# Adding the last routed batch into the output by accumulating transfers, unit by unit, instead of gathering it at the end

## What is computed

```python
x = x + 0.5 * _L1_ffn_ref(_layernorm(x, axis=-1), gate_w, w1, w2, w3)   # the last block, then return x

# _L1_ffn_ref: 8 experts, the 2 best of each token, at most 320 tokens of a batch for each expert
dispatch = einsum('bsm,bsec->ebcm', hidden_states, dispatch_mask)
h1 = einsum('ebcm,emh->ebch', dispatch, w1)
h3 = einsum('ebcm,emh->ebch', dispatch, w3)
expert_out = einsum('ebch,ehm->ebcm', silu(h1) * h3, w2)
final = einsum('ebcm,bsec->bsm', expert_out, combine_mask)
```

## Time and profile before

| | |
|---|---|
| median of 3 runs | 875.42 us (875.26 to 875.46) |
| the profiled execution's own time | 876.98 us |
| its span, first to last instruction | 875.2 us |
| PE busy in the span | 740.4 us (85%) |
| DVE, ACT, POOL busy | 503.7, 551.9, 322.5 us |
| mean granted clock of TensorE | 0.948 |

### The profile page before, as it was taken

How to read it: one execution, slowest core, us unless ns; L and a number is a source line. 1 busy time by engine, 2 the same in 40 slices (tenths; PEclk the granted TensorE clock), 3 DMA queues, 4 the chain that set the end, 5 groups by cost and what they waited for, 6 DMA issues and landing times.

```text
span 875.2 us, 13632 instructions
## 1 busy us (share of the span) xinstructions
PE 740.4 (85%) x4304; PEld 393.6 (45%) x4304; DVE 503.7 (58%) x1483; ACT 551.9 (63%) x960; POOL 322.5 (37%) x352
## 2 busy tenths in 40 slices
PE   5799999989999879858889797998988958789981
PEld 1432222212232225535555464775766845456650
DVE  6876532115655748622657299786897957223341
ACT  5368987989989866422466776867867515234440
POOL 3090003301001424263123475664763831634343
PEclk9899999999999999988999998998999969889996
DMA  4057651621881211111210200000000011111313
GB/s 127 1 194 177 146 118 46 224 67 49 293 171 53 85 42 39 36 45 36 71 35 18 68 1 1 1 1 1 1 1 1 31 47 30 56 38 51 91 44 92
DMA packets 63372, 57.55 MB, mean 66 GB/s; under 512 B 8260, under 2 KB 51385, under 8 KB 63040
## 3 DMA queue, kind: packets, MB, share of 16 engines
q1 hardware_dynamic: 57888, 47.84, 19.7%
q0 software_dynamic: 5120, 8.68, 3.0%
q10 hardware_dynamic: 288, 0.10, 0.0%
HBM read 28.64 MB, written 29.05 MB: 66 GB/s over the span
## 4 chain that ended last, share of the span: by engine, by line
PE 29%; DVE 11%; issue 8%; POOL 6%; ACT 4%; DMA 2%; another core or an unknown queue 2%; SPq 0%; POOLq 0%; DVEq 0%; ACTq 0%
PE ps_main L1628 11%; PE ps_main L1658 7%; PE ps_side L1946 3%; DVE mb_act L1982 2%; PE ps_main L2014 1%; POOL moe_slots L1555 1%; PE ps_main L1589 1%; PE ps_main L1624 1%; DVE moe_hid L1653 1%; POOL mb_z L2158 1%; DMA moe_back<-moe_rows 1%; POOL mb_y_in L2156 1%; PE ps_main L1699 1%; POOL mb_h_dec L2100 1%
## 5 line engine op out<-in xcount | busy, mean ns | idle before, releaser
L685 ACT ACTIVATE attn_p<-attn_ps 128x1024 f32<-128x1024 f32 x256 | 240.6, 1057 | 35.3 <-PE attn_ps L701 22.7
L1628 PE MATMUL ps_main<-moe_xsT,moe_w 128*128 128x320 f32 x384 | 132.1, 473 | 24.9 <-DVE moe_hid L1653 18.3
L701 PE MATMUL attn_ps<-attn_p,attn_v 128*32 128x512 f32 x1024 | 137.4, 608 | 4.1 <-issue 3.9
L1653 DVE TENSOR_TENSOR moe_hid<-moe_act_h,ps_main 128x320 f32<-128x320 f32 (+1 forms) x128 | 62.0, 486 | 117.4 <-ACT moe_act_h L1638 56.2
L1638 ACT ACTIVATE moe_act_h<-ps_main 128x320 f32<-128x320 f32 (+1 forms) x128 | 55.0, 434 | 118.0 <-PE ps_main L1628 58.1
L1555 POOL DMA_INDIRECT moe_slots<-rows,moe_scatter_at x64 | 64.0, 1000 | 98.7 <-issue 30.7
L1628 PEld LDWEIGHTS ps_main<-moe_xsT,moe_w 128*128 128x128 f32 x384 | 71.2, 202 | 60.1 <-issue 40.7
L678 PE MATMUL attn_ps<-attn_q_rows,attn_k_rows 64*128 64x512 bf16 x448 | 84.5, 388 | 11.7 <-ACT attn_p L685 5.0
L678 PEld LDWEIGHTS attn_ps<-attn_q_rows,attn_k_rows 64*128 64x128 bf16 x448 | 20.3, 93 | 134.6 <-ACT attn_p L685 119.0
L1658 PE MATMUL ps_main<-moe_hid,moe_w 128*128 128x320 f32 (+1 forms) x256 | 75.2, 465 | 4.1 <-DVE moe_hid L1653 4.1
L1726 POOL DMA_INDIRECT moe_rows<-moe_y,moe_dest x48 | 46.2, 962 | 85.6 <-ACT moe_y L1719 63.0
(11 more groups left out here) (264 smaller groups left out, 1354.5 us busy)
## 6 DMA issues: line engine op xcount, KB each, us to landing
moe_slots<-zeros SPq DMA_DIRECT2D x4, 1380.0 KB, 12.6
attn_q_rows<-attn_q_parts SPq DMA_DIRECT2D x36, 128.0 KB
attn_k_rows<-attn_k_parts SPq DMA_DIRECT2D x36, 128.0 KB
moe_w<-in_w SPq DMA_DIRECT2D x3, 1536.0 KB, 11.3
moe_rows<-zeros SPq DMA_DIRECT2D x4, 1024.0 KB, 15.0
moe_back<-moe_rows SPq DMA_DIRECT2D x16, 256.0 KB, 3.3
attn_q_parts<-attn_parts SPq DMA_DIRECT2D x4, 768.0 KB, 4.0
attn_k_parts<-attn_parts SPq DMA_DIRECT2D x4, 768.0 KB, 6.0
```

Of the source, the lines that this page charges most:

```text
L685: self.core.nc.scalar.activation(self.p[:, w % self.PB, :, :].rearrange("p a n -> p (a n)"), self.ps_s[:, w % self.SB, :, :].rearrange("p ...
L701: ins = self.core.nc.tensor.matmul(self.ps_av[32 * i:32 * i + 32, :], self.v[:, b * TPB + kt, HGROUPS * i + m, :], self.p[:, w % self.PB, ...
L1628: self.core.nc.tensor.matmul(ps[:, w % 2, 0:CAP], wt[:, e, c * P:(c + 1) * P], self.xsT[:, u % 2, :], start=True, stop=True).then_inc(self ...
L1653: self.core.nc.vector.tensor_tensor(self.hid[rows, u % 2, c, :], self.act_h[rows, w % 2, :], bank[rows, w % 2, 0:CAP], ALU.mult)\
```

## The change

It concerns batch 1 of the last block, units 24 to 31.

- Its x is stored to the output early, by SP behind the load of unit 20, after the Mamba block's last addition to x (L2405 to L2409 of the old text are gone).
- `send` of these units no longer writes to `moe_rows` but adds its rows to the output in DRAM, by an indirect transfer with `compute_op=ALU.add`. Two units may name the same output row, so each waits until the transfers of the unit before have landed. The first of them, unit 24, waits until all four stores of x have landed, those of batch 0 too.
- `address` gives these units the row `token + 1024` of the output (which holds batch 0 in rows 0 to 1023). A slot without a token points to a row of batch 0, one for each partition, and adds 0 there; no bounds check is used. The constants for that come from one new instruction on DVE at the start of the second half of the program.
- The fetch of batch 0 moves ahead of the load of unit 28 (it stood behind it), its combine from behind unit 29's `address` to chunks 1 and 2 of unit 27, and its two stores to behind the load of unit 29.
- The fetch, combine and store of batch 1 at the end are gone; SP waits for the stores and for the last transfers.
- Units 28 and 29 are no longer paired; `turn_back` and `weigh` of unit 30 move into chunk 2 of unit 31.
- The fourth `moe_rows` buffer and its clearing (1 MB of zeros) are gone.

```diff
-                sp.wait_ge(moe.cleared, 16 * 2 * 2 * B)
+                sp.wait_ge(moe.cleared, 16 * (2 * 2 * B - 1))
...
-    PAIRED = (0, 1, 2, 4, 5, 6, 8, 9, 10, 11, 12, 13, 14)
+    PAIRED = (0, 1, 2, 4, 5, 6, 8, 9, 10, 11, 12, 13)
...
+    def adds(self, u):
+        return u // E_ == 2 * B - 1
...
+        if self.adds(u):
+            nc.vector.tensor_scalar(self.second[:, at, :], row[:, :, self.TOKEN], float(T), self.unused_row[:], ALU.is_ge, ALU.mult).then_inc(self.chain, 1)
+            nc.vector.tensor_copy(self.weight[:, at, :], row[:, :, self.PROB + e]).then_inc(self.chain, 1)
+            dve.wait_ge(self.chain, 2 * u + 3)
+            nc.vector.scalar_tensor_tensor(self.dest[:, at, :], row[:, :, self.TOKEN], float(T), self.second[:, at, :], ALU.add, ALU.add).then_inc(self.sent, 1)
+            return
...
     def send(self, pool, u):
         pool.wait_ge(self.y_read, 3 * (u + 1))
         pool.wait_ge(self.sent, u + 1)
+        if self.adds(u):
+            if self.adds(u - 1):
+                pool.wait_ge(self.y_out[(u - 1) % self.OUT], 48 * ((u - 1) // self.OUT + 1))
+            else:
+                pool.wait_ge(self.core.stored, 16 * 2 * B)
+            for s, (c0, n) in enumerate(self.CHUNKS):
+                self.core.nc.gpsimd.indirect_dma_start(self.core.out_rows, bass.IndirectOffsetOnAxis(self.dest[0:n, u % self.OUT, s:s + 1], 0),
+                                                       self.y[u % self.OUT][0:n, s, :], None, compute_op=ALU.add)\
+                    .then_inc(self.y_out[u % self.OUT], 16)
+            return
...
-                        if c == 2 and u % 2 == 0 and u > HALF and moe.paired(u - 1):
+                        if c == 2 and u % 2 == 0 and u > HALF:
                             moe.results_odd(pe, u - 1, FCH * u + 2)
+                        if c == 2 and u == 2 * HALF - 1:
+                            moe.turn_back(pe, u - 1)
...
-                moe.turn_back(pe, 2 * HALF - 2)
                 moe.results_odd(pe, 2 * HALF - 1, FCH * 2 * HALF)
...
-                    if u in (E_ + 3, HALF + E_ + 4):
+                    if u in (E_ + 3, HALF + E_ + 3):
                         moe.fetch(sp, u // E_ - 1)
...
-                for half in range(2):
-                    sp.wait_ge(moe.combined, 2 * 2 + half + 1)
-                    sp.dma_start(core.stored_rows(0, half), core.x[:, half * GROUP:(half + 1) * GROUP, :]).then_inc(core.stored, 16)
-                moe.fetch(sp, 3)
-                for half in range(2):
-                    sp.wait_ge(moe.combined, 2 * 3 + half + 1)
-                    sp.dma_start(core.stored_rows(1, half), core.x[:, TPB + half * GROUP:TPB + (half + 1) * GROUP, :]).then_inc(core.stored, 16)
+                    if u == HALF + 4:
+                        sp.wait_ge(mamba.out_read, mamba.OUTS)
+                        for half in range(2):
+                            sp.dma_start(core.stored_rows(1, half), core.x[:, TPB + half * GROUP:TPB + (half + 1) * GROUP, :]).then_inc(core.stored, 16)
+                    if u == HALF + E_ + 5:
+                        for half in range(2):
+                            sp.wait_ge(moe.combined, 2 * 2 + half + 1)
+                            sp.dma_start(core.stored_rows(0, half), core.x[:, half * GROUP:(half + 1) * GROUP, :]).then_inc(core.stored, 16)
                 sp.wait_ge(core.stored, 16 * 2 * B)
+                for i in range(moe.OUT):
+                    sp.wait_ge(moe.y_out[i], 48 * 2 * HALF // moe.OUT)
...
+                        if u == HALF + E_ + 3 and c in (1, 2):
+                            moe.combine(dve, ch, 2, c - 1)
                     moe.address(dve, u)
-                    if u == HALF + 13:
-                        for half in range(2):
-                            moe.combine(dve, ch, 2, half)
-                for half in range(2):
-                    moe.combine(dve, ch, 3, half)
```

More of the change, by code:

```diff
@@ L901, in _ @@
                 half_ffn.base(pool)
[L902 removed]
+                pool.wait_ge(moe.cleared, 16 * (2 * 2 * B - 1))
                 pool.wait_ge(numbered, B)
@@ L1599, in take, with set_unused_row @@
         nc.vector.tensor_copy(self.xsT[:, u % 2, :], self.ps_t[:, 0:CAP]).then_inc(self.t_read, 1)
+    def adds(self, u):
+        return u // E_ == 2 * B - 1
+    def set_unused_row(self, dve):
+        self.core.landed(dve, "moe_token")
+        self.core.nc.vector.tensor_scalar(self.unused_row[:], self.token[:, 0:1], -self.NOWHERE - float(T), None, ALU.add).then_inc(self.chain, 1)
     def address(self, dve, u):
@@ L2688, in _ @@
                             moe.keep(act, u - 1)
-                        if c in (2, 3) and u % 2 == 0 and u > HALF and moe.paired(u - 1):
-                            moe.keep(act, u - 4 + c)
+                        if c == 2 and u % 2 == 0 and u > HALF and moe.paired(u - 1):
+                            moe.keep(act, u - 2)
+                        if c == 3 and u % 2 == 0 and u > HALF:
+                            moe.keep(act, u - 1)
+                        if c == 2 and u == 2 * HALF - 1:
+                            moe.weigh(act, u - 1)
                         if u == HALF and c == 2:
@@ L2710, in macaron @@
         core.stored = core.sem("stored")
+        core.out_rows = out.rearrange("b t d -> (b t) d")
         core.stored_rows = lambda b, half: out[b].rearrange("(g j p) d -> p g j d", g=2, p=P)[:, half, :, :]
```

11 lines of the change are left out of this document (6 added, 5 removed).

## The result

The changed kernel takes **885.54 us** (median of 4 runs, 884.43 to 889.09); the kernel before, run beside it, 875.34 (4 runs, 873.03 to 875.46). The ratio is 1.0122, with a 95% interval of 1.0087 to 1.0157: **slower by 1.2%**, 10.2 us, where 2.8 us less were predicted. The profiled execution took 884.88 us, its span 883.1 us.

What follows compares the result with a forecast made beforehand. A tail of transfers, worth at most 10.0 us, bounded the kernel; a serial chain of eight rounds would replace it. -6.8 + 8e, with e = 0.5, gave -2.8 us: 872.6 us from 875.42, range 868.5 to 882.

Steps and rivals of the forecast that it cites:

- chain of eight rounds: Units 24 to 31, each waiting for the one before to land: 5.35 us a round plus e, setting the end.
- (a): In a round, from release to the start of the unit's first transfer: 0.77 us.
- e: Extra time of a round because its transfers add: 0.5 us taken, paid eight times, 4.0 us in all.
- the second, slower: Each adding transfer pays a second trip, behind each round's third transfer: 8e, slower from e = 0.85, up to 886.1 us; chance 0.30.
- (b): In a round, from the start of the first transfer to the start of the third: 2.56 us.
- The two bounds: Limits on e: 0 if the output read is hidden, 2.19 us for a whole read trip before the write.
- (c): In a round, from the start of the third transfer to its landing: 2.02 us for a plain scatter.
- The rule that was weighed: DMA reductions run half as fast as copies; doubling 1.05 us gives e = 1.05 and 877.0 us, some 0.08 chance.
- the closing: From the last landing to the end of the span: 0.75 us, before and after the change.
- load 28: Unit 28's load, moved behind batch 0's fetch, lands in 3.3 us and delays PE by 0.3 us, between 0 and 0.6.
- the net of -0.7 on PE: Everything on PE behind unit 30 comes about 0.7 us earlier, after load and combine delays and a removed 1.95 us wait.
- rival 3: DVE's stops called remote shift or change in number, moving the time up to 4 us either way, 868.6 to 876.6; chance 0.09.

Runs made afterwards that it cites:

- plain kernel: The changed kernel with spare slots dropped by a bounds check and batch 1's rows written without adding: 873.76 us, ratio 0.9979 against the kernel before.

## Why the prediction was wrong

**Right: what sets the end.** The chain of eight rounds stood alone in the tail, nothing on PE, ACT or DVE was late, and the last weighing on ACT ended at 854.5, some 17 us before unit 31 could be sent. The start was 13.8 us behind the fetch for 13.4. Batch 0's store landed in 2.32 us for 2.28, part (a) of a round is 0.77 to 0.78 for 0.77 (0.84 at the start of the chain), and DVE stood 2.3 us for unit 24's landing, which is near e, as the text said it would:

```profile
DVE moe_second L1623 <- DMA out<-moe_y,moe_dest: 4.2, 2, 2.3
PE ps_main L1591 <- DMA moe_xs<-moe_slots: 0.5, 1, 0.5
```

The rival that came nearest is the second, slower, and its counting holds: paid in each of eight rounds, decided from e = 0.85, and under its upper bound of 2.19, since e was 7.41 - 5.35 = 2.06. Its place, the landing behind the third transfer, holds for less than half of that.

**Wrong: the term e.** The step is "It does what the plain one does and reads 64 KB of the output besides". It made e a question of the transfer's path alone, taken at 0.5, and kept (b) at its plain 2.56. The two bounds were sought in landings. What grew most is the issuing, which the prediction had as a constant: (b) 3.72 us (3.78 in the first round, 820.24 to 824.02) for 2.56, (c) 2.85 to 2.98 for 2.02, of which 0.52 is the longer instruction again. Eight rounds make of it 8 x 1.56 = 12.5 us more than was forecast. The plain kernel shows that the rest of the working stands: with instructions of 0.97 us its rounds are 5.40 to 5.51, where the sum without e was 5.35.

**The rule that was weighed.** Behind the end of its instruction a 64-row plain transfer landed 2.02 - 0.91 = 1.1 us later, an adding one 2.86 - 1.43 = 1.43 in the changed kernel, and with a bounds check mostly 2.54 - 1.43 = 1.11. The Trainium skill ("Collectives: The Full Stack", section "The bandwidth ceiling: the fold count and why AG ≠ RS ≠ AR") has a reduction in the DMA engines at half a copy's rate, measured on large transfers. By it I had e = 1.05; this part grew by 0.3 to 0.4 us and didn't double, and e became 2.06 through something that the rule doesn't speak of. That the range reached 882, far enough for the chain alone, is owed to this rival, whose reason was not the one that came true: that was luck. The Trainium skill ("DMA: Bandwidth & Descriptors", section "Anatomy of one DMA — SWDGE (gpsimd) path") calls descriptor generation small beside the 2 us of a transfer. If POOL's instruction is that part, this case's rows speak against it: it is 0.91 of 2.02 us for a plain transfer, and 1.43 of 2.86 for an adding one.

**Wrong: the closing.** The step is "0.75 us of closing", read behind SP's last store in a kernel whose POOL had issued its last transfer 12 us earlier. When POOL issues last, the closing is its drain, 4.4 us behind the landing. That is 3.65 us, and without it the time would have been 881.9, inside the range that ended at 882. The row for it was in the trace before: DRAIN ends 868.6 - 862.41 = 6.2 us behind the start of POOL's last transfer. I had stopped at SP because the chain of waits did, and asked nothing of what else must end once that chain is gone.

**Wrong in size: load 28.** "Hence a delay of 0.3 us, with ends of 0 and 0.6": PE waited 0.5 us in the changed kernel and 0.7 to 1.4 in six more with the fetch ahead, since the load landed 3.60 to 4.42 us behind its second part's issue where the chain of waits shows it, for 3.3 taken. With it the net of -0.7 on PE was -0.3 in the kernel with only the fetch and the combine moved, and +1.3 with the new order too, 1.0 of it from unpairing. In the changed kernel it moved the chain's start by 0.4 us, 13.8 for 13.4.

**Open.** What the stops called remote are. They were rival 3, and one of 7.97 us stood in the profile after where the earlier trace rows had 4.28 and 3.75:

```profile
765.64 0.49 DVE L1672 TENSOR_TENSOR moe_hid<-moe_act_h,ps_main 128x320 f32<-128x320 f32 x1 [7.97 <-remote]
```

The stretch ahead of the tail was 806 to 812 us in executions of both kinds of kernel on the first chips, and 783 to 788 on the last, where no wait is called remote; it doesn't go with the change. Why it varies wasn't tried. It also leaves the small gains of the order (0.2 to 0.4%) known only to their intervals.

## What to carry over

Before a fetch and store at the end is replaced by accumulating transfers, multiply the whole cost of one, its issuing included, by the number of links that must follow each other; adding in place makes a serial chain out of transfers that could overlap, and here each of 8 links grew by 2.1 us where all that could be removed was a tail of 10 us. When a change makes another engine the last to issue, look up when that engine's program really ends in the old trace, since its end may have been hidden there. A step that must go into a busy engine's stream costs nothing only in a gap that the timeline shows: the same four additions cost PE 1.95 us behind unit 29's `address`, 0.8 in unit 27 and nothing behind chunk 2 of unit 28.

## What was not expected of the hardware

- An accumulating indirect transfer occupies POOL for 1.56 us with 128 rows and 1.43 with 64, a plain one 0.97 and 0.91; and it has more packets, 2176 for 24 transfers.
- POOL's DRAIN at the end of the program ends 5.3 us after the last indirect instruction does, adding or not: 882.55 against 875.82 + 1.43, 868.6 against 862.41 + 0.91, and, in the plain kernel, 875.2 against 868.96 + 0.91. It is 5.2 to 5.4 us in all thirteen traces, some 4 us after the transfer has landed.
- A unit's load issued right behind the fetch of 1 MB lands up to 4.4 us after its issue; elsewhere such a load takes 2.19.
- The kernel before differs by some 20 us between chips (874 and 854.5). The three traces from the faster chip reach the tail about 20 us earlier and have none of the waits of up to 9.6 us that the others call remote; what these are the traces can't say.
